# Order of the four matmuls of a gate, up or down group: high parts of both banks, then low parts of both

## The reference

```python
# convolution: one kernel of length 1024 per head h, made from log_dt, C, A; tokens past the length are masked
y = irfft(rfft(u * mask) * rfft(kernel)) [..., :L] + u * mask * D      # times mask
# feed-forward on 2048 tokens of width 1024, INTER = 2752, groups of 128 rows share a scale
w[k, n] = q[k, n] * s[k // 128, n] - (z[k // 128, n] + 1) * s[k // 128, n]
mid = silu(y @ Wg) * (y @ Wu)
out = x + mid @ Wd
```

## Time and profile before

| | |
|---|---|
| median of 3 runs | 1258.28 us |
| lowest, highest | 1256.48, 1259.15 us |
| the profiled execution | 1258.08 us |
| its span, first to last instruction | 1256.3 us |
| mean granted clock of PE | 0.973 of full |
| PE busy | 1171.2 us, 93% |
| PEld busy | 956.1 us, 76% |
| DVE busy | 915.1 us, 73% |
| ACT busy | 844.8 us, 67% |
| POOL busy | 237.3 us, 19% |

### The profile page before, as it was taken

The page is one execution under the profiler, slowest core; times in us unless marked ns, Lnnn a source line. Parts: engine busy times, 40 slices in busy tenths (PEclk is TensorE's granted clock), DMA queues, the critical chain, the costliest instruction groups (busy, mean ns, idle before and its releaser), DMA issues.

```text
span 1256.3 us, 15416 instructions
## 1 busy us (share of the span) xinstructions
PE 1171.2 (93%) x5546; PEld 956.1 (76%) x5546; DVE 915.1 (73%) x915; ACT 844.8 (67%) x1383; POOL 237.3 (19%) x133
## 2 busy tenths in 40 slices
PE   2389899999999999999999979999999999999994
PEld 2389899867878878788787767878878878788772
DVE  8975672367777777777777778877777777777777
ACT  2342120388878788787887867777878788788862
POOL 5402110012121121211212374112121121211211
PEclk9689899999999999999999989999999999999996
DMA  5365556373443434434334246465343433434504
GB/s 174 106 241 203 170 204 244 115 187 100 110 109 91 122 99 103 115 93 120 99 104 113 71 108 175 130 202 171 99 118 95 119 100 102 116 93 119 142 9 192
DMA packets 147618, 162.79 MB, mean 130 GB/s; under 512 B 24710, under 2 KB 110918, under 8 KB 147542
## 3 DMA queue, kind: packets, MB, share of 16 engines
q1 hardware_dynamic: 147510, 161.78, 45.1%
q0 software_dynamic: 32, 0.03, 0.0%
HBM read 152.92 MB, written 8.82 MB: 129 GB/s over the span
## 4 chain that ended last, share of the span: by engine, by line
PE 81%; DVE 12%; issue 2%; DMA 2%; SPq 2%; ACT 1%; POOL 0%; DVEq 0%
PE pair L1034 24%; PE pair L1049 24%; PE pair L1065 24%; PE pair L993 8%; DVE acc L862 1%; SPq L379 1%; DVE p L619 1%; DMA x_fin<-in_x_dram 1%; DVE s_r L619 1%; DVE q_in L809 1%; DVE t L615 1%; DMA z_in<-zeros_plus_one 1%; DVE th_l L712 0%; PE pair L977 0%; DVE turns L717 0%
## 5 line engine op out<-in xcount | busy, mean ns | idle before, releaser
L862 DVE SCALAR_TENSOR_TENSOR acc<-pair,s_down,acc 128x1024 f32<-128x1024 f32 x336 | 431.0, 1283 | 216.9 <-PE pair L1065 216.7
L558 ACT ACTIVATE pair<-pair,ratio 128x512 f32<-128x512 f32 x616 | 383.1, 668 | 123.5 <-PE pair L1034 123.5
L577 ACT ACTIVATE pair<-pair,ratio 128x512 f32<-128x512 f32 x588 | 365.4, 661 | 130.8 <-PE pair L1049 130.8
L1034 PE MATMUL pair<-xs,wg 128*128 128x512 f32 x1408 | 391.8, 400 | 7.8 <-issue 5.3
L1049 PE MATMUL pair<-xs,wu 128*128 128x512 f32 x1344 | 372.2, 399 | 1.8 <-DVE sil L846 1.8
L1034 PEld LDWEIGHTS pair<-xs,wg 128*128 128x128 f32 x1408 | 263.4, 189 | 78.1 <-issue 7.4
L1049 PEld LDWEIGHTS pair<-xs,wu 128*128 128x128 f32 x1344 | 249.4, 189 | 69.0 <-issue 11.7
L1065 PE MATMUL pair<-mid_h,wd 128*128 128x512 f32 x704 | 279.6, 401 | 7.2 <-DVE acc L862 4.5
L1065 PE MATMUL pair<-mid_l,wd 128*128 128x512 f32 x672 | 263.9, 393 | 0.0
L469 POOL CAST mid_h<-sil 128x1024 fp32r<-128x1024 f32 (+1 forms) x44 | 45.7, 1039 | 869.5 <-DVE sil L846 851.2
L1065 PEld LDWEIGHTS pair<-mid_h,wd 128*128 128x128 f32 x704 | 133.0, 190 | 44.6 <-DVE acc L862 10.8
(11 more groups left out here) (149 smaller groups left out, 445.7 us busy)
## 6 DMA issues: line engine op xcount, KB each, us to landing
z_in<-zeros_plus_one SPq DMA_DIRECT2D x130, 256.0 KB, 4.6
toep<-kernel_padded SPq DMA_DIRECT2D x64, 512.0 KB, 4.3
q_in<-_L_ffn_gate_qweight_dram SPq DMA_DIRECT2D x336, 64.0 KB, 2.3
q_in<-in_L_ffn_up_qweight_dram SPq DMA_DIRECT2D x336, 64.0 KB, 2.2
q_in<-_L_ffn_down_qweight_dram SPq DMA_DIRECT2D x42, 512.0 KB, 5.7
toep<-in_x_dram SPq DMA_DIRECT2D x16, 512.0 KB, 4.3
x_fin<-in_x_dram SPq DMA_DIRECT2D x12, 512.0 KB, 7.9
out_dram<-x_fin SPq DMA_DIRECT2D x12, 512.0 KB, 6.9
```

Of the source, the lines that this page charges most:

```text
L558: act.activation(gate_ps[:, tb, :], gate_ps[:, tb, :], ACT.Copy, scale=ratio[:, 0, G * t + g:G * t + g + 1]).then_inc(gate_scaled, 1)
L577: act.activation(up_ps[:, tb, :], up_ps[:, tb, :], ACT.Copy, scale=ratio[:, 1, G * t + g:G * t + g + 1]).then_inc(up_scaled, 1)
L862: dve.scalar_tensor_tensor(out=acc[:, hid, :], in0=ps, scalar=scale, in1=acc[:, hid, :], op0=ALU.mult, op1=ALU.add).then_inc(down_taken, 1)
L1034: mm = pe.matmul(gate_ps[:, tb, :], w["g"][tau % 2][:, g, :], xs[:, part, g, 512 * tb:512 * tb + 512], start=g == 0 and part == 0, stop=pa ...
```

## The change

In `gate`, `up` and `down` the loop over the parts is now the outer one. The four matmuls of a group come as high part of bank 0, high part of bank 1, low part of bank 0, low part of bank 1; before it was high and low of bank 0, then high and low of bank 1. The waits stand before the first matmul into each bank, so the wait for bank 1 stands ahead of the second matmul of the group, where it stood ahead of the third. The counts for ACT stand on the third and the fourth matmul, where they stood on the second and the fourth. The number of matmuls, weight loads, waits and counts is the same. A down of a tail tile keeps its order.

```diff
-                for tb in range(2):
-                    if G * tau + g:
-                        pe.wait_ge(gate_scaled, 2 * (G * tau + g) - 1 + tb)
-                    for part in range(2):
+                for part in range(2):
+                    for tb in range(2):
+                        if part == 0 and G * tau + g:
+                            pe.wait_ge(gate_scaled, 2 * (G * tau + g) - 1 + tb)
                         mm = pe.matmul(gate_ps[:, tb, :], w["g"][tau % 2][:, g, :],
                                        xs[:, part, g, 512 * tb:512 * tb + 512],
                                        start=g == 0 and part == 0, stop=part == 1, skip_group_check=g > 0)
-                    mm.then_inc(gate_mm, 1)
+                        if part == 1:
+                            mm.then_inc(gate_mm, 1)
...
-                for tb in range(2):
-                    for part, mid in enumerate(parts):
+                for part, mid in enumerate(parts):
+                    for tb in range(2):
                         mm = pe.matmul(down_ps[at % 2][:, tb, :], w["d"][tau % 2][:, P * hid:P * hid + P],
```

More of the change, by code:

```diff
@@ L1044, in up @@
                         pe.wait_ge(mid_done, tau)
-                for tb in range(2):
-                    if g:
-                        pe.wait_ge(up_scaled, 2 * ((G - 1) * full_before(tau) + g) - 1 + tb)
-                    for part in range(2):
+                for part in range(2):
+                    for tb in range(2):
+                        if part == 0 and g:
+                            pe.wait_ge(up_scaled, 2 * ((G - 1) * full_before(tau) + g) - 1 + tb)
                         mm = pe.matmul(up_ps[:, tb, :], w["u"][tau % 2][:, g, :],
@@ L1051, in up @@
                                        start=g == 0 and part == 0, stop=part == 1, skip_group_check=g > 0)
-                    mm.then_inc(up_mm, 1)
+                        if part == 1:
+                            mm.then_inc(up_mm, 1)
             def down(tau, hid):
```

## The result

| | before | changed |
|---|---|---|
| median of 20 runs | 1259.06 us | 1263.08 us |
| lowest, highest | 1256.48, 1262.81 | 1257.77, 1264.71 |
| profiled execution | 1258.08 | 1261.59 |
| its span | 1256.3 | 1259.7 |

The ratio is 1.0023, with a 95% interval of 1.0012 to 1.0033: slower by a quarter of a per cent, 2.9 us. It follows the means (1259.17 and 1262.01 us). The medians lie further apart, by 4.0 us, because the changed kernel's times fall in two groups: 9 runs from 1257.8 to 1261.6 and 11 from 1263.1 to 1264.7. The profiled execution is one of the lower group. The forecast was 1.7 us, and the range of 1255.5 to 1264.5 holds the median. The spread of both kernels is wider than the three runs of before had let me think.

The account below looks back on a forecast made before the run. PE was taken to bound the kernel, busy 93% of the span, with matmuls 0.233 us apart in either bank order. The profiled 1258.08 + 1.5 (tile 43) + 0.2 (tile 21) gave 1259.8 us, range 1255.5 to 1264.5.

Parts of the forecast that it names:

- Twelve matmuls, cost nothing: Full steps, some 300: ACT starts the up pair 0.23 us later, with 0.40 us to spare; cost nothing.
- A: A change of bank costs more than staying: 7 ns on 2048 distances, +14 us, 1272; chance 0.08.
- rival C: The shift reaches the full steps after all: at 20 ns a step +6 us, 1264; chance 0.10.
- B: A change of bank costs less than staying: 3 ns on 2048 distances, -6 us, 1252; chance 0.12.
- the 70 us by the Trainium skill's 216 ns: If the 17 ns over 216 were a price of returning to the same bank, 4128 matmuls would save 70 us.
- Tile 43, +1.5 us: Last tail, steps of eight matmuls: second weight load 0.34 us late, 0.22 lost in each of 7 steps, +1.5 us.
- D: Nothing moves the end: the 0.34 us of tile 43 is caught up or covered by DVE; 1258.1; chance 0.18.
- Ten matmuls and tile 0, cost nothing: Ten matmuls (8 steps): load 0.06 us late, caught up. Tile 0: ACT the bound, 0.16 to spare. Cost 0.
- Tile 21, +0.2 us: Eight matmuls, ACT the bound: groups end 0.23 us later, less 0.04 of slack, paid once through DVE, +0.2 us.
- The forecast's own bounds: Forecast's own range, 1258.1 to 1261.2 us (2.4 + 0.2 + 0.5), with +-1.3 of run spread on top; chance 0.52.

Follow-up runs that it names:

- the kernel with the race taken away: Changed kernel, but POOL's first split for the second half (tile 21) waits for DVE's unpacking of tile 22's weights; 1260.03 us, ratio 1.0004.
- before without the loads: Kernel before, leaving out four of the loads of x for the first half's output (transfers 4 to 7); 1256.82 us, ratio 0.9985.

## Why the prediction was right, and where it was wrong

- **Twelve matmuls, cost nothing.** Right: tiles 2 to 20 differ by 0.1 us in 426.6. The 0.40 us to spare was enough, and rivals A and C, 14 and 6 us, fall with it. So does B: a change of bank has no price of its own and no gain, and with it the 70 us by the Trainium skill's 216 ns (TensorE: Matmul & The Clock Gate, "Back-to-back issue gap"). That section of the Trainium skill has the 216 ns as the gap of an isolated matmul and gives about 131 ns for a stream of weight loads and matmuls. The 0.233 us measured here is neither.
- **Tile 43, +1.5 us.** Right in mechanism, a little too large: 1.23 us up to the tile's multiply, in all four traces with the new order there. The steps are 2.04 to 2.07 us against the 2.08 worked out, but six are longer and not seven. The first group of the tile has no new wait, and the last one's lateness is covered by DVE's queue of work. The load was shown waiting 0.36 to 0.39 us, of which some 0.2 was lost. The +1.5 from this tile on matches by luck, since 0.3 of it lies behind the multiply. D, that nothing moves, falls.
- **Ten matmuls and tile 0, cost nothing.** Tile 22's steps of ten are 2.32 and 2.33 us, as before. Tile 0 was 0.2 us longer, the 0.23 that the prediction names and prices at nothing; tile 1 varies by 3 us from trace to trace, so whether it reaches the end isn't shown.
- **Tile 21, +0.2 us.** The step that failed. DVE does take each group later, and it is busy without a hole from there, but two things were missed. First, the prediction calls ACT the bound in all eight steps. The second and third took 1.86 and 1.87 us before, where steps that ACT bounds take 2.10, and each was stretched by 0.2; so the wait itself is worth 0.4, as the kernel with the race taken away shows. Second, the sum took DVE's instructions at fixed lengths. The trace of before had line 809 at 0.77 us next to 1.71 and 1.67 in the same tile, which I had read as length and not as a race. The 0.2 us turned a lead of 0.18 us into a lag of 0.01, and the term measures 1.36 us. With it the traces have 1.23 + 1.36 = 2.6 us from tiles 43 and 21. The 2.9 us of the ratio are near that, but with an interval from 1.5 to 4.2 us they do not prove the sum.
- **The rest of the profiled difference.** The 1.3 us in tiles 22 and 23 and the 1.1 us in tiles 24 to 28 are in that one execution: the second race, and a wait for x that is there with both orders. The first stage, which the change doesn't touch, was 1.6 us shorter and takes back two thirds of them; it goes from 237.5 to 240.0 us over the twelve traces.
- **The range and the chances.** I gave 0.30 to slower by over 0.2% and 0.58 to no change. At 0.23% the result lies just beyond the line, on the side that had 0.30; by the medians it is 0.32%. The forecast's own bounds, 1261.2 us and 1.3 of spread, do not reach the median of 1263.08. The range holds it because rival C had lent it 1264.5, and C did not happen, so that is luck. The spread of +-1.3 us came from three runs; 20 runs of before reach over 6.3 us. In the traces the first stage, tile 1 with its clock, the race in tile 22 and the late transfer differ by 1 to 4 us each.

## What to carry to other kernels

Before a wait is moved by one matmul, work out for each kind of step when the awaited engine is done and when the moved instruction is due; the full steps had 0.4 us to spare, and eight short ones of the tails, of 352, were stretched. Where the same instruction has two lengths in one trace, look for the engine that runs beside it: a shift of 0.2 us can change who goes first, and be worth seven times itself. Judge such an effect tile by tile in the trace, up to an instruction behind which nothing has changed, since a difference of 3 us in the median is of the size of the spread.

## What the runs showed of the hardware

- The pitch of 512-column matmuls, each with its own weight load, is 0.233 us whether the next one goes to the same PSUM bank or to another: 426.65 and 426.55 us for 19 tiles.
- A DVE unpacking of 128x1024 int32 took 0.74 to 0.77 us alone or when it began ahead of POOL, and 2.87 to 2.94 us when POOL's 2.4 us instruction had begun 0.01 or 0.06 us ahead of it; a two-input one took 1.21 and 2.24 us. The blocked instruction is shown as long, not as waiting.
- A weight load that waits 0.36 to 0.39 us in a flowing group costs some 0.2 us, and the loads behind it come closer together (three in 0.53 us; 0.65 in a flowing group).
- The granted clock differs between executions of the same instructions: from 256 to 268 us it was 0.86 in before and 0.72 in before without the loads, which is the same program up to there, with tile 1 at 22.77 and 24.22 us.
